# A graph layer with 24 neighbour slots per graph in place of 44, and one slot for left-over neighbours

## The reference

```python
scores = jnp.where(mask, -jnp.arange(N), -jnp.inf)
vals, idx = jax.lax.top_k(scores, 25)
feats = jnp.where(valid[..., None], X[idx], -jnp.inf)
agg = feats.max(axis=2)
agg = jnp.where((degree <= 25)[..., None], jnp.maximum(agg, 0.0), agg)
x = x + relu(concat([X, agg]) @ W + b)          # X = layernorm(x)
x = x + ffn(layernorm(x))                       # 2 layers, 16 experts, 1 shared
```

## Time and profile before

| what | value |
|---|---|
| timed runs | median 737.73 us (736.75 to 739.88, three runs) |
| profiled execution, span from first to last instruction | 734.5 us (no total of its own is recorded) |
| busy: PE, PEld | 611.5 us (83%), 502.9 us (68%) |
| busy: DVE, POOL, ACT | 574.2 us (78%), 541.9 us (74%), 521.2 us (71%) |
| chain that ended last, by engine | PE 59%, DVE 22%, issue 5% |
| DMA moved | 131.73 MB, mean 179 GB/s |

### The profile page before, as it was taken

One profiled execution on the slowest core, in us unless ns is written; L12 is line 12 of the kernel. 1 busy time (PEld: TensorE's weight loads), 2 busy tenths in 40 slices (PEclk: granted clock), 3 DMA queues, 4 the chain that ended last, 5 costly groups with the idle time before them and its releaser, 6 DMA issues.

```text
span 734.5 us, 11755 instructions
## 1 busy us (share of the span) xinstructions
PE 611.5 (83%) x3496; PEld 502.9 (68%) x3497; DVE 574.2 (78%) x959; ACT 521.2 (71%) x981; POOL 541.9 (74%) x388
## 2 busy tenths in 40 slices
PE   0466666679999799979997999899987999799686
PEld 0054545566987588858885888668875988588565
DVE  3766799878987898779987898789878987777740
ACT  5672455369977898779876987699769985478062
POOL 4577488497979987898878897989799878984000
PEclk9986798898999899979998999989998999799989
DMA  9999997479746965496638755785474543045222
GB/s 298 305 196 265 314 344 241 134 176 293 226 132 158 267 175 152 102 259 205 166 109 222 236 163 142 190 240 159 127 182 124 161 138 87 22 113 144 58 72 77
DMA packets 145171, 131.73 MB, mean 179 GB/s; under 512 B 72219, under 2 KB 112324, under 8 KB 145092
## 3 DMA queue, kind: packets, MB, share of 16 engines
q1 hardware_dynamic: 128124, 105.94, 53.5%
q0 software_dynamic: 7296, 15.74, 8.3%
q10 hardware_dynamic: 9680, 9.21, 4.5%
HBM read 98.20 MB, written 17.98 MB: 158 GB/s over the span
## 4 chain that ended last, share of the span: by engine, by line
PE 59%; DVE 22%; issue 5%; DVEq 4%; DMA 4%; ACT 4%; SPq 1%; ACTq 0%
PE slot_ps L777 28%; PE ffn_ps L842 11%; DVE acc L988 9%; PE ffn_ps L852 4%; PE ffn_ps L826 4%; PE prep_ps L869 3%; DMA at<-mask 2%; PE ffn_ps L811 2%; PE ffn_ps L792 2%; DVEq L1060 2%; DVE top L1047 2%; PE ffn_ps L812 2%; DMA adj_sb<-in_adj_dram 2%; DVE wst L1153 1%; DVE score L1049 1%
## 5 line engine op out<-in xcount | busy, mean ns | idle before, releaser
L777 PE MATMUL slot_ps<-onehot,xsplit 128*128 128x512 f32 (+3 forms) x1376 | 375.5, 401 | 51.1 <-DVE acc L988 44.4
L988 DVE TENSOR_TENSOR acc<-slot_ps,acc 128x896 f32<-128x896 f32 (+2 forms) x336 | 293.7, 884 | 77.3 <-PE slot_ps L777 74.5
L547 POOL TENSOR_SCALAR onehot<-rank,ranks 128x896 fp32r<-128x896 bf16 (+3 forms) x128 | 298.4, 2333 | 72.6 <-PE slot_ps L777 67.5
L777 PEld LDWEIGHTS slot_ps<-onehot,xsplit 128*128 128x128 f32 x1376 | 251.9, 204 | 105.7 <-issue 71.0
L535 POOL DMA_INDIRECT gath<-feature_table,idx x200 | 207.7, 1038 | 47.9 <-issue 42.6
L842 PE MATMUL ffn_ps<-hT,wst 128*128 128x128 f32 x1024 | 135.1, 277 | 0.0
L842 PEld LDWEIGHTS ffn_ps<-hT,wst 128*128 128x128 f32 x1024 | 129.0, 191 | 5.9 <-issue 0.8
L670 ACT ACTIVATE away<-rank,ranks 128x896 bf16<-128x896 bf16 (+4 forms) x136 | 107.9, 793 | 6.8 <-DVE wst L1153 6.4
L687 ACT ACTIVATE onehot<-away 128x896 fp32r<-128x896 bf16 (+4 forms) x136 | 96.3, 708 | 21.5 <-PE slot_ps L777 10.6
L629 ACT ACTIVATE hT<-ffn_ps,wst 128x128 f32<-128x128 f32 x256 | 81.1, 375 | 29.5 <-PE ffn_ps L842 27.3
L641 ACT ACTIVATE rank<-prep_ps 128x448 bf16<-128x448 f32 x128 | 63.0, 550 | 21.0 <-PE prep_ps L869 11.7
(11 more groups left out here) (121 smaller groups left out, 586.3 us busy)
## 6 DMA issues: line engine op xcount, KB each, us to landing
wst<-folded_weights SPq DMA_DIRECT2D x128, 257.0 KB, 2.9
adj_sb<-in_adj_dram SPq DMA_DIRECT2D x64, 512.0 KB, 5.9
folded_weights<-wst ACTq DMA_DIRECT2D x34, 256.0 KB, 6.9
hT<-in_L_ffn_Wr_dram SPq DMA_DIRECT2D x26, 256.0 KB, 10.3
xs<-in_x_dram SPq DMA_DIRECT2D x8, 512.0 KB, 8.1
feature_table<-xn SPq DMA_DIRECT2D x8, 512.0 KB, 4.1
x<-in_x_dram SPq DMA_DIRECT2D x8, 512.0 KB, 4.3
out_dram<-h SPq DMA_DIRECT2D x16, 256.0 KB, 2.4
```

The lines of the kernel that those rows point to most:

```text
L547: pool.tensor_scalar(onehot[:, UNIT[n]:UNIT[n] + many, 0:wide * P], rank[:, b % 2, first:first + many, 0:wide * P], ranks[:, r - 1:r], Non ...
L777: mm = pe.matmul(slot_ps[n % 2][:, c0:c1], xsplit[:, b % 2, part, first + j, :], onehot[:, UNIT[n] + j, c0:c1], start=(j == 0 and part == ...
L988: dve.tensor_tensor(acc[:, p % 2, 0:cols], slot_ps[n % 2][:, 0:cols], acc[:, p % 2, 0:cols], ALU.max).then_inc(s_max, 1)
```

## The change

The 44 slots become 24, with eight groups of one tile each and smaller capacities. They stand at 24 of the 44 positions (`TURN_POS`), with two more turns between them, `ORDERED` and `LEFT`. What exceeds a capacity is taken up per graph by a new chain. `of_tile`, `earlier` and `places` are constants that GpSimd sets up at the start.

- The last row of `rank` (each node's neighbours per tile) goes by one DMA to 56 partitions (`totals`, position 40); VectorE subtracts the capacities (`count`, 43), TensorE sums over neighbour tiles (1), VectorE flags nodes above them (2), TensorE numbers the flagged nodes by a prefix sum (4), VectorE makes a matrix that puts node number i on partition i (5), TensorE finds each listed node and its capacities with it (7), VectorE makes row indices (8).
- GpSimd loads the adjacency rows of the up to 128 listed nodes by an indirect DMA (`left_rows`, 9). VectorE scores them, ScalarE makes a mask (15), SP transposes it (16), and in the turn `ORDERED` (23) TensorE ranks the neighbours within each tile, VectorE keeps those above the capacity and takes the eight with the lowest index (`keep_left`).
- GpSimd gathers six of them per node (26 to 31), VectorE takes their maximum (35), ScalarE and GpSimd split it in two parts (36, 37), and the turn `LEFT` (43) multiplies it with a one-hot matrix of the listed nodes; the result is folded as a slot's.
- `judge` takes the place of `check_totals`. Rank matmuls of a second tile in a group go. `xs` has one buffer instead of two, `away` one instead of two; the load of the next graph's `x` moves on SP from position 12 to 17.

```diff
-GROUPS = [(0, 1), (1, 1), (2, 1), (3, 1), (4, 1), (5, 2), (7, 1)]
-CAPS = [[10, 9, 8, 7, 7, 7, 7],
...
+LISTED = 6
+CAPS = [[6, 6, 5, 5, 4, 4, 4],
+        [4, 3, 3, 3, 3, 3, 3],
+        [3, 3, 3, 3, 3, 2, 2],
+        [3, 3, 3, 2, 2, 2, 2],
+        [2, 2, 2, 2, 2, 2, 2],
...
+LEFT_ADJ_AT = 9
+LEFT_MASK_AT = 15
+LEFT_TURN_AT = 16
+LEFT_GATHER_AT = {26: 0, 27: 1, 28: 2, 29: 3, 30: 4, 31: 5}
+LEFT_MAX_AT = 35
...
+            def left_rows(b):
+                pool.wait_ge(s_noderow, b + 1)
...
+                pool.indirect_dma_start(left_adj[:, :], None, adj_rows,
+                                        bass.IndirectOffsetOnAxis(ap=node_row[:, 0:1], axis=0)
+                                        ).then_inc(s_leftadj, 16)
...
+            def left_gather(b, j):
+                pool.wait_ge(s_leftidx, b + 1)
...
+            def left_mask_of(b):
+                act.wait_ge(s_leftadj, 16 * (b + 1))
...
+                if q == Q_ORDERED:
+                    pe.wait_ge(s_leftturn, 16 * (b + 1))
+                    if n >= 2:
+                        pe.wait_ge(s_max, n - 1)
+                    for jt in range(NG):
+                        mm = pe.matmul(slot_ps[n % 2][:, jt * P:(jt + 1) * P], left_at[:, jt, :], before[:, :],
+                                       start=True, stop=True)
...
+            def keep_left(b):
+                n = b * NT + Q_ORDERED
+                dve.wait_ge(s_slot, n + 1)
+                dve.wait_ge(s_leftscore, b + 1)
+                for jt in range(NG):
+                    part = left_score[:, jt * P:(jt + 1) * P]
+                    ins = dve.scalar_tensor_tensor(out=part, in0=slot_ps[n % 2][:, jt * P:(jt + 1) * P],
+                                                   scalar=least[:, jt:jt + 1], in1=part, op0=ALU.is_gt, op1=ALU.mult)
+                ins.then_inc(s_max, 1)
...
+                if p == LEFT_MASK_AT:
+                    dve.wait_ge(s_leftadj, 16 * (b + 1))
...
+            def count(b):
+                dve.wait_ge(s_totals, 16 * (b + 1))
...
+                    rows = left_split[:, part, :] if q == Q_LEFT else xsplit[:, b % 2, part, TURNS[q][0], :]
```

More of the change, by code:

```diff
@@ L780, in slot @@
-                mm.then_inc(s_slot, 1)
+                for part in range(PARTS):
+                    rows = left_split[:, part, :] if q == Q_LEFT else xsplit[:, b % 2, part, TURNS[q][0], :]
+                    for c0 in range(0, wide * P, BANK):
+                        c1 = min(c0 + BANK, wide * P)
+                        mm = pe.matmul(slot_ps[n % 2][:, c0:c1], rows, onehot[:, unit(n), c0:c1],
+                                       start=(part == 0), stop=(part == PARTS - 1))
+                mm.then_inc(s_slot, 1)
```

512 lines of the change are left out of this document (338 added, 174 removed), and 5 rows, old and new, of the table PLACES.

## The result

The changed kernel takes 728.98 us (median of 4 runs, 724.6 to 732.36) beside 737.24 us for the kernel before: a ratio of 0.990, 95% interval 0.985 to 0.994. It is faster by 1%, where 683 us was forecast, and outside the forecast range (656 to 718).

What follows compares the result with a forecast made beforehand. Three engines at 68 to 72 us were taken to bound a 77.7 us stage, GpSimd fullest afterwards. From 734.5 us, minus 47 (six stages), minus 9 (last slot stage), plus 1 (start), plus 3.2 for timed runs: 683 us, range 656 to 718.

Steps and rivals of the forecast that it cites:

- The loads: Repeated stage: TensorE 58.7 us, VectorE 59.1 (62.2 with drains), GpSimd 63.8 with its gaps, ScalarE near 51.
- I leave the same 6 us on top: Repeated stage: 6 us beyond the fullest engine, as before, because engines run in order and wait for each other.
- the forecast 69.8: Repeated stage: 69.8 us with the new chain, 7.9 us less, 47 us in six stages.
- The 6 us of slack above are what pays for these hand-overs: New chain in every stage: its hand-overs between engines fit in the 6 us left on top.
- Last stage with slots: 613 to 686.4 us: 64 us, 9 us less, with 6 us on top and 3 for the chain's tail.
- Start and weight stage: 0 to 147 us: +1 us; set-up 3 to 4 later, VectorE 7 less, 4 given back for late DMA.
- Last stage: The last 48.1 us, which have no slots, stay unchanged.
- The first, blocked small steps: VectorE's small steps wait 2.0 us each for GpSimd one-hots: 76 us a stage, 725 us (705 to 733); chance 0.12.
- The second, a late row load: Position 15: row load landing beyond 8.5 us delays VectorE and ScalarE; 775 us at 20 us; chance 0.07.
- The third, the clock: TensorE's mean clock falls to 0.75, its work 73.6 us, a stage 77: 727 us; chance 0.06.
- The fourth: TensorE is the bound again and GpSimd's gaps close up: stage 64.7 us, 650 us; chance 0.08.
- fifth: Nodes over the limits make the change fall back to redoing them one tile at a time; no chance left.

Runs made afterwards that it cites:

- e1: Changed kernel without the whole left-over chain (24 slots stay, left-over neighbours missing from the output): 659.0 us, 0.897 of the kernel before.
- e9: Changed kernel with ScalarE's high part moved from position 36 to 39 and GpSimd's low part from 37 to 40: 759.8 us, 1.036 of the kernel before.
- e4: Changed kernel with list, search and row load behind the normalisation, the chain's later links also later, one slot moved: 756.0 us, 1.027 of the kernel before.
- e5: Changed kernel with three ScalarE adjacency masks and the second group of normalised rows at earlier positions: 720.6 us, 0.978 of the kernel before.
- e16: Changed kernel with maximum's parts on VectorE, gathers at 26 to 28, maximum at 33, early masks, later search, three slots moved to first half: 713.6 us, 0.970.
- e18: As e16, but the maximum's parts on ScalarE and GpSimd and five slots moved to the first half: 710.8 us, 0.966 of the kernel before.
- e13: Changed kernel with VectorE making both parts of the gathered maximum at position 35, not ScalarE and GpSimd: 745.9 us, 1.011 of the kernel before.
- e11: As e10, with find, found and row load moved from positions 7, 8, 9 to 9, 10, 11: 751.6 us, no ratio given.
- e10: Changed kernel with the edits of e5 and e9 together: 760.1 us, 1.032 of the kernel before.
- e3: Changed kernel with only the front of the left-over chain; row load through last slot removed: 667.8 us, 0.907 of the kernel before.
- e2: Changed kernel with only the back of the left-over chain; totals through find removed, constant rows loaded: 707.6 us, 0.963 of the kernel before.

## Why the prediction was wrong, point by point

**The loads were right.** Forecast for a repeated stage: TensorE 58.7 us, VectorE 59.1, ScalarE near 51. Measured: 60.2, 60.7 and 53.4. GpSimd's 63.8 included the gaps ahead of its gathers; it is busy 56.5 and these gaps make 7.0 (17.8 and 3.3 in three stages), 63.5 together.

**The step that failed is "I leave the same 6 us on top".** The stage is 13.3 us above its fullest engine, GpSimd with its gaps (76.8 and 63.5). Without any chain there are already 11.3: e1's stage is 69.3 and its TensorE, the fullest there, busy 58.0 (173.9 us in three stages). The average over the stage hid that it has two halves with different limits. TensorE's saved work was counted whole; 5 of it lay in the first half, which is as long as the feed-forward chain of one graph. That e1 lands on the forecast 69.8 is chance: a stage with the chain was meant.

**"The 6 us of slack above are what pays for these hand-overs" failed with it.** The chain costs 7.5 us in a repeated stage (76.8 and 69.3). Its steps lengthen the first half by 3.8 us in the means and the second by 3.7. That the order of the links costs, whatever the engines' work, is shown by the runs that moved links and left the loads: three positions for two small steps cost 31 us (e9), two to four positions for the chain 27 us (e4), and three masks and a group of rows moved ahead gained 8 (e5). How much of the 7.5 us is order is not shown: in the second half, which TensorE nearly fills, its own work is 1.8 to 2.4 us more in the stages above than in e1's, and the best orders found (e16 to e18) still take 74.6 to 75.1 us a stage.

**Last stage with slots:** 9 us less forecast, 4.5 measured (73.4 and 68.9). Without the chain it takes 58.9 us, so the slots gave 14.5, as forecast (14.4), and the chain took 10.0 in place of 4.8. **Start and weight stage:** +1 forecast, +1.8 measured, by two terms far larger than forecast that cancel: e1 starts its first input transposes at 134.4 us, before at 146.8, the changed kernel at 148.6. **Last stage:** forecast unchanged, 49.6 against 48.3.

**Rivals.** The first, blocked small steps, gave a time that fits (705 to 733). It priced the steps as load, 70.2 us a stage on VectorE, and there it is wrong: VectorE is busy 60.7. But steps are blocked, and they stand on the chain that sets the first half. The list's seven compares, at the same place of the stages that begin at 227.0 and 302.0 us, and the one-hot beside the second:

```profile
237.56 1.23 DVE L1185 TENSOR_SCALAR left_at<-number,place 128x128 bf16<-128x128 f16 x7
```

```profile
312.38 2.55 POOL L635 TENSOR_SCALAR onehot<-rank,ranks 128x896 fp32r<-128x896 bf16 x1
```

```profile
312.56 2.98 DVE L1185 TENSOR_SCALAR left_at<-number,place 128x128 bf16<-128x128 f16 x7
```

No one-hot ran beside the first. The normalisation ends 19.75 us after the first of these stages began and 21.50 after the second, and their first halves are 37.8 and 40.3 us. Of the six stages two are of the first kind (37.8 us both); in the four others the compares take 1.6 to 3.0 us, the first counting step takes 1.1 where it takes 0.2 and 0.5 in those two, and the first halves are 39.7 to 40.3. One step of the normalisation, which the rival did not name, takes 1.50 us in all six stages (the row at 398.78 above), beside GpSimd's row load and one-hot; before:

```profile
L964 DVE TENSOR_SCALAR newton<-newton x10: 171/174/175, 11.5 to 697.4; 128x16 f32<-128x16 f32 x6, 128x8 f32<-128x8 f32 x4
```

Together they would make some 2.5 of the 3.8 us by which the chain lengthens the first half (an estimate: 1.3 in each stage, 1.8 in four of six). That is not tested: no run takes the blocking out alone, e13 has first halves of up to 41.4 us with unblocked compares, and in e11 the step of the normalisation takes 0.17 us while the half stays where e10 has it (38.9 and 39.0). The index steps, which took 2.25 us before, now take 0.23. By the Trainium skill, page "SBUF — State Buffer", section "SBUF: two separate sides", VectorE in some of its modes and GpSimd share a port pair, and the one that holds it blocks the other for a whole instruction. The changed kernel's trace agrees in the counting step, which ran from 379.51 to 380.60 us and ended 0.08 us behind a GpSimd one-hot (from 377.98, 2.54 us); it does not in the step of the normalisation, which ended at 400.28 us, 1.5 ahead of the end of the one-hot beside it. The second, a late row load, did not happen: it lands in 4.2 to 10.2 us, and neither VectorE nor ScalarE waits for it. The third, the clock, is at most a part: the granted clock of three stages is 0.90 where it was 0.94, far from the rival's 0.75, and no run sets it by itself. The fourth and fifth did not happen.

**Left open.** How the chain's 7.5 us divide among its links, since no link was taken out alone in the back; and why front and back together cost 12 us more than the two apart. A candidate for the second, untested, is the blocking: in e3, the front alone, the list's compares take 1.23 us in every stage, and in e2 and e3 the step of the normalisation takes 0.17 us in every repeated stage (in the weight stage of e3 0.87).

## What to carry to other kernels

A load per engine, averaged over a loop's round, tells what a change is worth only where the round has one limit. Cut the round at the points where the waits change, and ask of each piece whether it is full or a chain through several engines; work removed from engines that wait for a chain gives next to nothing (0.4 us of a first half here, for 5 to 10 us of work on each of three engines). A serial chain added to engines that run in order is priced by its place: look at what stands behind each link on its engine, and try the links' positions before counting on slack. Price a small step by what runs beside it, and by whether it stands on the chain, not by its share of its engine's load.
